# Four graph layers over a dense adjacency: int32 narrowed to bytes by GpSimd's converting transfers

## Chip, cores, metric

One core of a Trainium2 chip runs the whole program. The metric is device time in microseconds, median of the runs of a kernel. One further execution was profiled; every row quoted below is from it.

## What is computed

The input is x (8 graphs, 2048 nodes, 128 features, float32) and adj (8, 2048, 2048, int32, entries 0 or 1, each 1 with probability 0.0039). Four layers follow, each as x = x + layer(relu(layernorm(x)), adj):

```python
# layer 0: attention with 8 heads of 32, then one head of 128
e   = leaky_relu(f1[..., :, None] + f2[..., None, :], 0.2)
att = softmax(where(adj > 0, e, -9e15)); hp = elu(att @ h)      # twice, plus the input
# layer 1: maximum over a node's neighbours (itself left out)
cand = where(adj_without_diagonal > 0, h[:, None, :, :], -1e30)
out  = relu(norm(h @ W_self + cand.max(axis=2) @ W_neigh))
# layer 2: attention with 4 heads of 32
# layer 3: mean over the nodes that point here
pooled = (adj.T @ h) / counts;  out = leaky_relu(h @ B + pooled @ W, 0.1)
```

So all four layers of a graph need its adjacency: as a byte mask (layers 0, 2, 3) and as lists of each node's neighbours (layer 1).

## The kernel before

**Tiles.** A graph's adjacency is 16 tiles of 128 rows by 2048 columns, 1 MB a tile as int32. In SBUF it is held as bytes twice: `A` (rows) and `AT` (transposed), 16 tiles each.

**The load of a graph** (`load`, L382 to L390 on SyncE; `cast`, L760 to L772 on ScalarE; `transposed` on TensorE; `take` on VectorE). SyncE moves an int32 tile into one of two halves of the buffer `Rb` (L390), after a wait until ScalarE has done with that half. ScalarE reads it twice: L769 writes a bf16 copy and sums the row (the degree), L771 writes the byte copy with the value 56 into `A`. TensorE transposes the bf16 copy in 16 pieces (L1486), VectorE writes it to `AT` (L1148). `Rb` is also where the attention heads' rows lie, so SyncE begins a load only when the heads of layer 2 have ended. The loads of graphs 0 and 1 stand alone; those of graphs 2 to 7 are interleaved, one pair of tiles at a time, with the last layer of the graph two before.

**The software pipeline** (`pipeline`, L290). For each step b: `beside(b+1, b)` is the single wide head of layer 0 of graph b+1 with layer 1 of graph b woven in; `middle(b)` is layer 2 of graph b; `last_layer(b, b+2)` is layer 3 of graph b with the load of graph b+2; `heads_of(b+2)` is the eight heads of layer 0 of graph b+2. At the end come `beside(None, 7)`, `middle(7)` and `last_layer(7)`.

**The lists.** While the heads run, VectorE finds each node's neighbours eight at a time (`list_tile`, reading `A`), and SyncE or ScalarE stores the found numbers to DRAM (`lists`).

**The gather** (`gather`, L602 to L613, GpSimd). For each graph and each of its 16 tiles GpSimd fetches index lists (L543), fetches 128 rows per index with indirect transfers (L551, eight to a round, from `table` in DRAM, which holds layer 1's input), and takes maxima (L534 to L537); L595 writes the tile's result to `Agg`. GpSimd begins the gather of graph b when `table` has been written (semaphore `tab_in`, at the end of `beside(b, ...)`) and adds 1 to `maxima` at its end (L613). TensorE waits for `maxima` in `sage_arrived` (L1364), which in `sums` (L1379) comes after the second of the 16 tiles of `beside(b+1, b)`. One gather therefore runs beside all of `middle(b-1)`, `last_layer(b-1, b+1)`, `heads_of(b+1)` and the start of `beside(b+1, b)`.

All instructions of an engine run in the order written. GpSimd's queue of transfers is made by its software; SyncE's and ScalarE's are made by hardware. All three are moved by the same 16 DMA engines.

Of the kernel before, what the change touches and what calls it, by code (L numbers as in the profile page):

```python
# [31 lines left out]
ACT = mybir.ActivationFunctionType  # L32
# [3 lines left out]
U8, I8, U32, I32 = mybir.dt.uint8, mybir.dt.int8, mybir.dt.uint32, mybir.dt.int32  # L36

P = 128
# [5 lines left out]
ONE8 = 56  # L44
# [18 lines left out]
def build(nc, x, adj, W1, a1, W2, a2, Wself, bself, Wneigh, bneigh, gamma, beta, WC, aC, W3, B3, out):  # L63
    B, N, F = x.shape
    T = N // P
# [18 lines left out]
    with ExitStack() as ctx:  # L84
        def sb(name, shape, dt=F32):
            return ctx.enter_context(nc.sbuf_tensor(name, shape, dt))

        def sem(name):
            return ctx.enter_context(nc.semaphore(name))


        A = sb("A", [P, T, N], U8)
# [14 lines left out]
        Rb = sb("Rb", [P, 2, N])  # L107
# [20 lines left out]
        deg = sb("deg", [P, T])  # L128
# [23 lines left out]
        found_idx = sb("found_idx", [P, KEYS], U32)  # L152


        stage_i32 = Rb[:, :, :].bitcast(I32)
        f1row, f2row = Pbuf[0:8, 0, :], Pbuf[0:8, 1, :]
        xc = xcbuf[:, :].rearrange("p (t c) -> p t c", t=T)
        Dg = xcbuf[:, T * F:T * F + T * F // 2].bitcast(BF16).rearrange("p (t c) -> p t c", t=T)
        stage_bf = Pbuf[:, 0, :].bitcast(BF16).rearrange("p (u n) -> p u n", u=2)
# [25 lines left out]
        x1 = nc.dram_tensor("x1", [B, P, T * F], F32, kind="Internal").ap()  # L185
        h1 = nc.dram_tensor("h1", [B, P, T * F], F32, kind="Internal").ap()
        bytes_A = nc.dram_tensor("bytes_A", [B * T, P, N], U8, kind="Internal").ap()
        bytes_AT = nc.dram_tensor("bytes_AT", [B * T, P, N], U8, kind="Internal").ap()
        lists = nc.dram_tensor("lists", [ROUNDS + 2, P, KEYS], U32, kind="Internal").ap()
        h0 = nc.dram_tensor("h0", [P, T * F], F32, kind="Internal").ap()  # L190
# [17 lines left out]
        AT_in = sem("AT_in")  # L208
        adj_in = [sem("adj_in0"), sem("adj_in1")]
        cast_done = sem("cast_done")  # L210
        bf_done = sem("bf_done")
        at_ps = sem("at_ps")
        at_done = sem("at_done")
# [27 lines left out]
        keyed = sem("keyed")  # L241
# [9 lines left out]
        M = {m: {k: sem(f"{m}_{k}") for k in ("T", "hT", "W", "ev", "y")} for m in ("sage", "pool")}  # L251
# [15 lines left out]
        def plain(eng):  # L267

            eng.wait_ge(ready, 1)

        def settle(eng):

            eng.sem_inc(settled, 1)
# [43 lines left out]
        def _(sp):  # L317
# [22 lines left out]
            def tile_of(buffer, t):  # L340
                return buffer[:, bass.ds(t, 1), :].rearrange("p o c -> p (o c)")
# [39 lines left out]
            def load(b, alone):  # L381
                with sp.Fori(0, T // 2) as tt:  # L382
                    for u in range(2):
                        rows = x[bass.ds(b, 1), bass.ds(tt * (2 * P) + u * P, P), :].rearrange("o p f -> (o p) f")
                        sp.dma_start(tile_of(X, tt * 2 + u), rows).then_inc(x_in, 16)

                        plain(sp)
                        sp.wait_ge(cast_done, b * T + tt * 2 + (u + 1))
                        src = adj[bass.ds(b, 1), bass.ds(tt * (2 * P) + u * P, P), :].rearrange("o p n -> (o p) n")
                        sp.dma_start(stage_i32[:, u, :], src).then_inc(adj_in[u], 16)  # L390

            def heads_of(b, alone):

# [94 lines left out]
            def last_layer(b, following, alone):  # L488
                if following is not None:

                    plain(sp)
                    sp.wait_ge(S[LC]["pe"], b * (LC.H * T) + LC.H * T + free_P[LC])
                    settle(sp)
                    load(following, False)
                plain(sp)
                sp.wait_ge(x_done, b + 1)
                sp.dma_start(out[bass.ds(b, 1)].rearrange("o (t p) f -> p (o t) f", p=P), X2[:, :, :]).then_inc(out_done, 16)

            sp.sem_inc(out_done, 16)
            pipeline(sp, load, heads_of, beside, middle, last_layer)  # L500
            sp.wait_ge(out_done, B * 16 + 16)


        @block.gpsimd
        def _(pool):
# [33 lines left out]
            def fetch(r, slot):  # L539

                plain(pool)
                pool.wait_ge(list_in, r * 16 + 32)
                pool.dma_start(idx[:, slot, :], lists[bass.ds(r, 1)].rearrange("o p k -> (o p) k")).then_inc(idx_in[slot], 16)  # L543
# [11 lines left out]
            def number(b, t):  # L555
                return pool.value_load(cum[0:1, bass.ds(b * (T + 1) + t, 1)], min_val=0, max_val=ROUNDS)

            def tile(b, t, last):
                lo, hi = number(b, t), number(b, t + 1)

                fetch(lo if last else lo + 1, 1)
                rows_of(b * T + t + 1, 0, best)
                if last:

                    plain(pool)
                    pool.wait_ge(idx_in[1], lo * 16 + 16)
                pool.sem_inc(merged, MERGE)  # L570
                with pool.Fori(lo + 1, hi) as r:
                    if last:
                        fetch(r, 1)
                    rows_of(r + 1 if last else r, 1, G)
                    v = Chain(pool, merged, r * MERGE, MERGE)
                    for half in range(2):

                        plain(pool)
                        for k in range(half * KEYS // 2, (half + 1) * KEYS // 2):
                            pool.wait_ge(got[k], r * 16 + 16)  # L580
                        if half == 1 and not last:

                            fetch(r + 1, 1)
                        part = slice(half * KEYS // 2, (half + 1) * KEYS // 2)
                        greater(v, best[:, part, :], G[:, part, :])
                    v.end()
                    settle(pool)
                if not last:

                    fetch(hi, 0)  # L590
                v = Chain(pool, tree, (b * T + t) * TREE, TREE)
                for width in (4, 2, 1):
                    greater(v, best[:, 0:width, :], best[:, width:2 * width, :])
                settle(pool)
                v(pool.tensor_copy(Agg[:, bass.ds(t, 1), :].rearrange("p o f -> p (o f)"), best[:, 0, :]))  # L595
                v.end()
                if not last:

                    plain(pool)
                    pool.wait_ge(idx_in[1], hi * 16)  # L600
                settle(pool)

            def gather(b):

                plain(pool)

                pool.wait_ge(tab_in, b * 16 + 16)
                settle(pool)
                fetch(number(b, 0), 0)
                with pool.Fori(0, T - 1) as t:  # L610
                    tile(b, t, False)
                tile(b, T - 1, True)
                pool.sem_inc(maxima, 1)  # L613

            gather(0)
            if B > 1:
                with pool.Fori(0, B - 1) as b:

                    plain(pool)
                    pool.wait_ge(M["sage"]["T"], b * T + T)  # L620
                    gather(b + 1)


        @block.scalar
        def _(act):
# [135 lines left out]
            def cast(b, tt):  # L761

                for u in range(2):
                    n = b * T + tt * 2 + u
                    plain(act)
                    act.wait_ge(adj_in[u], (b * (T // 2) + tt + 1) * 16)

                    act.wait_ge(at_ps, n + 1)
                    act.activation(stage_bf[:, u, :], stage_i32[:, u, :],  # L769
                                   ACT.Copy, accum_out=deg[:, bass.ds(tt * 2 + u, 1)]).then_inc(bf_done, 1)  # L770
                    act.activation(A[:, bass.ds(tt * 2 + u, 1), :], stage_i32[:, u, :].rearrange("p (o n) -> p o n", o=1),  # L771
                                   ACT.Copy, scale=float(ONE8)).then_inc(cast_done, 1)  # L772

            def load(b, alone):
                with act.Fori(0, T // 2) as tt:
                    cast(b, tt)
# [775 lines left out]
```

## Time and profile before

| | before |
|---|---|
| median of 3 runs | 9315.55 us (9288.4 to 9319.17) |
| profiled execution, its own time | 9293.71 us |
| its span | 9292.0 us |
| mean granted clock of TensorE | 0.800 |
| TensorE busy | 5501.9 us (59%) |
| VectorE busy | 5998.1 us (65%) |
| ScalarE busy | 4627.4 us (50%) |
| GpSimd busy | 5119.1 us (55%) |
| bytes moved by DMA | 629.10 MB, mean 68 GB/s |

Busy time is the sum of an engine's instructions without its waits. No engine is busy over two thirds of the span, so the waits tell what bounds a stage: for each, the profile infers which instruction of another engine released it. The chain that ended last is followed back from the last instruction through these releases.

### The profile page before, as it was taken

The page shows a single profiled execution, that of the slowest core. Times are in us where ns is not written, and L with a number is a line of the kernel's source. Part 1 is how long each engine was busy: PE and PEld are TensorE (multiplying, and loading weights), DVE is VectorE, ACT ScalarE, POOL GpSimd, SP SyncE. Part 2 cuts the span into 40 slices and gives each one's busy share as a digit, 9 for nine tenths or more (in the row PEclk, how much of TensorE's full clock was granted, in tenths as well). Part 3 has the DMA queues.
Part 4 walks back from the last instruction along what each step waited for, and adds up shares of the span by engine and source line. Part 5 has one row for each costly group of instructions (what it writes and reads, how often), then busy time and mean ns, then how long its engine had stood idle before and what let it go on. Part 6 is the DMA issues. An engine that isn't in the chain of part 4 may idle for free.

```text
span 9292.0 us, 189286 instructions
## 1 busy us (share of the span) xinstructions
PE 5501.9 (59%) x62584; PEld 4902.1 (53%) x62584; DVE 5998.1 (65%) x7394; ACT 4627.4 (50%) x4624; POOL 5119.1 (55%) x5234
## 2 busy tenths in 40 slices
PE   3764670365776668564875668565775667562037
PEld 2663670363765547463864557454764557461026
DVE  4874871385876778685866778586866778581024
ACT  5643650165744557264845566355735566260034
POOL 0003777376753777376754676176764677277720
PEclk9886885687887889787987889787887888786568
DMA  2114332134332433235322533134323533222210
GB/s 97 38 38 109 68 71 24 31 69 124 61 65 58 105 79 61 50 64 134 65 59 66 120 65 75 51 63 107 66 60 67 119 64 77 56 52 55 27 22 28
DMA packets 305343, 629.10 MB, mean 68 GB/s; under 512 B 113273, under 2 KB 163962, under 8 KB 268666
## 3 DMA queue, kind: packets, MB, share of 16 engines
q0 software_dynamic: 91936, 161.87, 16.6%
q1 hardware_dynamic: 210514, 456.38, 13.9%
q8 instruction: 584, 9.57, 0.4%
q14 instruction: 149, 1.22, 0.0%
q10 hardware_dynamic: 2160, 0.06, 0.0%
HBM read 506.89 MB, written 111.15 MB: 67 GB/s over the span
## 4 chain that ended last, share of the span: by engine, by line
DVE 29%; PE 23%; issue 13%; ACT 7%; POOL 3%; DVEq 3%; DMA 2%; ACTq 2%; POOLq 0%; SPq 0%
PE ps L1419 7%; DVE keys L1095 4%; PE ps L1421 3%; PE ps L1444 3%; DVE key L1085 3%; PE ps L1333 3%; ACT Pbuf L700 2%; PE ps L1392 2%; PE ps L1330 2%; DVE key L1071 2%; ACT Hn L700 2%; DVE Hn L955 2%; DVE Zs L975 1%; DVE Zs L976 1%; DVE AT L1148 1%
## 5 line engine op out<-in xcount | busy, mean ns | idle before, releaser
L1421 PE MATMUL ps<-Hn,AT 128*128 128x99 bf16 x12288 | 1773.1, 216 | 0.0
L551 POOL DMA_INDIRECT G<-table,idx x1416 | 1493.0, 1054 | 504.4 <-issue 444.9
L1421 PE MATMUL ps<-X,AT 128*128 128x99 bf16 x12288 | 1738.0, 215 | 15.3 <-issue 15.3
L543 POOL DMA_DIRECT2D idx<-lists x433 | 259.3, 599 | 2644.6 <-issue 2164.8
L700 ACT ACTIVATE Hn<-Rb,q 128x2048 int8<-128x2048 f32 x768 | 1485.0, 1988 | 98.0 <-PE ps L1421 94.1
L700 ACT ACTIVATE Pbuf<-Rb,q 128x2048 int8<-128x2048 f32 x768 | 1487.2, 1987 | 12.7 <-PE ps L1421 10.3
L551 POOL DMA_INDIRECT best<-table,idx x1024 | 1109.0, 1083 | 319.5 <-issue 309.4
L1419 PE MATMUL ps<-X,Hn 128*128 128x198 bf16 x6144 | 938.2, 269 | 553.4 <-DVE Hn L955 318.1
L1421 PEld LDWEIGHTS ps<-Hn,AT 128*128 128x128 fp8e4 x12288 | 1256.3, 102 | 0.0
L1421 PEld LDWEIGHTS ps<-X,AT 128*128 128x128 fp8e4 x12288 | 1244.8, 101 | 16.5 <-issue 16.5
L1419 PE MATMUL ps<-Hn 128*128 128x198 bf16 x6144 | 960.3, 272 | 428.7 <-DVE Zs L975 243.1
L1419 PEld LDWEIGHTS ps<-X,Hn 128*128 128x128 fp8e4 x6144 | 652.4, 106 | 583.8 <-issue 567.0
L1419 PEld LDWEIGHTS ps<-Hn 128*128 128x128 fp8e4 x6144 | 660.5, 108 | 468.0 <-issue 448.2
L1419 PE MATMUL ps<-Hn,Pbuf 128*128 128x198 bf16 x6144 | 831.6, 252 | 66.0 <-DVE Pbuf L955 65.8
L1419 PE MATMUL ps<-X,Pbuf 128*128 128x198 bf16 x6144 | 820.0, 250 | 25.0 <-DVE Pbuf L955 25.0
L955 DVE SCALAR_TENSOR_TENSOR Hn<-Hn,AT 128x512 int32<-128x512 int32 x768 | 628.6, 847 | 216.5 <-ACT Hn L700 148.8
L955 DVE SCALAR_TENSOR_TENSOR Pbuf<-Pbuf,AT 128x512 int32<-128x512 int32 x768 | 633.6, 853 | 159.5 <-ACT Pbuf L700 126.9
L1095 DVE MAX8 keys<-key 128x8 f32<-128x2056 f16 x305 | 701.3, 2299 | 33.8 <-DVE key L1085 8.9
L1419 PEld LDWEIGHTS ps<-Hn,Pbuf 128*128 128x128 fp8e4 x6144 | 606.2, 99 | 79.3 <-issue 77.0
L729 ACT ACTIVATE hT<-ps 128x512 f32<-128x512 f32 x64 | 38.2, 597 | 1180.0 <-PE ps L1350 1180.0
L1419 PEld LDWEIGHTS ps<-X,Pbuf 128*128 128x128 fp8e4 x6144 | 601.9, 98 | 30.4 <-issue 29.8
L882 DVE COPY WHbuf<-ps 128x128 f32 (+1 forms) x384 | 129.1, 336 | 738.8 <-PE ps L1333 738.8
(190 smaller groups left out, 11639.4 us busy)
## 6 DMA issues: line engine op xcount, KB each, us to landing
Rb<-in_adj SPq DMA_DIRECT2D x128, 1024.0 KB
Rb<-rrows SPq DMA_DIRECT2D x104, 1024.0 KB, 6.5
bytes_A<-A SPq DMA_DIRECT2D x128, 256.0 KB
bytes_AT<-AT SPq DMA_DIRECT2D x128, 256.0 KB
AT<-bytes_AT SPq DMA_DIRECT2D x128, 256.0 KB
AT<-bytes_A SPq DMA_DIRECT2D x128, 256.0 KB, 3.6
G<-table,idx POOLq DMA_INDIRECT x1416
h<-Hn SPq DMA_DIRECT2D x16, 1024.0 KB, 4.2
```

The lines of the kernel that those rows point to most:

```text
L543: pool.dma_start(idx[:, slot, :], lists[bass.ds(r, 1)].rearrange("o p k -> (o p) k")).then_inc(idx_in[slot], 16)
L551: pool.indirect_dma_start(out=dst[:, k, :], out_offset=None, in_=table, in_offset=bass.IndirectOffsetOnAxis(ap=idx[:, slot, k:k + 1], axis ...
L700: act.activation(marks[(u * T + jb) % RING].bitcast(I8), Rb[:, u, :], ACT.Sign, bias=q[:, jb, hs], scale=-1.0).then_inc(s["sg"], 1)
L955: dve.scalar_tensor_tensor(marks[k % RING], marks[k % RING], NO_SIGN, A32, ALU.bitwise_and, ALU.bitwise_and).then_inc(s["p"], 1)
L1071: v(dve.scalar_tensor_tensor(key[:, 0:N], A[:, bass.ds(t, 1), :].rearrange("p o n -> p (o n)"), 0.0, iota[:, :], ALU.is_gt, ALU.mult))
L1085: dve.match_replace(key[:, :], keys8[:, :], key[:, :], 0.0).then_inc(removed, 1)
L1095: dve.max(keys8[:, :], key[:, :]).then_inc(found, 1)
L1330: pe.matmul(ps[:, 2 + u, 0:W], hT[:, u, k, :], w["cat"][:, k, :], start=k == 0, stop=k == L.KB - 1)
L1333: ins = pe.matmul(ps[0:L.H, 4 + u, e * P:(e + 1) * P], wf[:, k, :], hT[:, u, k, :], start=k == 0, stop=k == L.KB - 1)
L1419: pe.matmul(both[:, :, 0:G], greater[:, at], v.rearrange("p (g x) -> p g x", g=2), start=first, stop=False, skip_group_check=True)
L1421: ins = pe.matmul(both[:, 0, 0:G], A8[:, jb, at], v[:, 0:G], start=False, stop=jb == T - 1, skip_group_check=True)
L1444: ins = pe.matmul(ps[:, 4 + u, 0:3 * F + 1], A8[:, k, (tt * 2 + u) * P:(tt * 2 + u + 1) * P], PS3[:, k, 0:3 * F + 1], start=k == 0, stop=k ...
```

## The change

A second DRAM tensor `adj8` holds the adjacency as bytes. GpSimd issues, tile by tile, a transfer from `adj` (int32) to `adj8` (uint8) in DRAM (`narrow`), with at most two in flight, one for each of the semaphores `narrowed0` and `narrowed1`. Those of graphs 0 and 1 (32 tiles) are issued at the program's start, after GpSimd's constants. Those of graph b+2 (16 tiles) are issued in `gather(b)` for b = 0 to 5, after `tab_in` has been waited for and ahead of the first fetch. SyncE's load moves 256 KB a tile from `adj8` straight into `A`; it waits for `narrowed` and for its own transfer of the pair before, and no longer for ScalarE. The first seven pairs wait until the lists of the graph before but the last tile's are found (`keyed`), the last pair until all are. ScalarE's two passes read the byte tile in `A` in place of `Rb`; the second writes it in place. Nothing of the arithmetic of the layers changes.

```diff
+        adj8 = nc.dram_tensor("adj8", [B * T, P, N], U8, kind="Internal").ap()
...
+        narrowed = [sem("narrowed0"), sem("narrowed1")]
...
+                def pair(tt):
+                    for u in range(2):
                         plain(sp)
-                        sp.wait_ge(cast_done, b * T + tt * 2 + (u + 1))
-                        src = adj[bass.ds(b, 1), bass.ds(tt * (2 * P) + u * P, P), :].rearrange("o p n -> (o p) n")
-                        sp.dma_start(stage_i32[:, u, :], src).then_inc(adj_in[u], 16)
+                        sp.wait_ge(narrowed[u], b * (T // 2 * 16) + tt * 16 + 16)
+                        settle(sp)
+                        if not (alone and isinstance(tt, int) and tt == 0):
+                            plain(sp)
+                            sp.wait_ge(adj_in[u], b * (T // 2 * 16) + tt * 16)
+                            settle(sp)
+                        sp.dma_start(tile_of(A, tt * 2 + u), of(adj8, b * T + (tt * 2 + u))).then_inc(adj_in[u], 16)
+
+                if not alone:
+                    plain(sp)
+                    sp.wait_ge(keyed, b * (3 * T) - 3)
+                    settle(sp)
+                pair(0)
+                with sp.Fori(1, T // 2 - 1) as tt:
+                    pair(tt)
...
+                pair(T // 2 - 1)
...
+            def narrow(b, t, u):
+                rows = adj[bass.ds(b, 1), bass.ds(t * P, P), :].rearrange("o p n -> (o p) n")
+                pool.dma_start(adj8[bass.ds(b * T + t, 1)].rearrange("o p n -> (o p) n"), rows).then_inc(narrowed[u], 16)
+
+            def gather(b, ahead):
                 plain(pool)
                 pool.wait_ge(tab_in, b * 16 + 16)
                 settle(pool)
+                if ahead:
+                    with pool.Fori(0, T // 2) as tt:
+                        for u in range(2):
+                            plain(pool)
+                            pool.wait_ge(narrowed[u], (b + 2) * (T // 2 * 16) + tt * 16)
+                            settle(pool)
+                            narrow(b + 2, tt * 2 + u, u)
                 fetch(number(b, 0), 0)
...
+            for b in range(min(B, 2)):
+                for t in range(T):
+                    if b * T + t >= 2:
+                        pool.wait_ge(narrowed[t % 2], (b * T + t) // 2 * 16)
+                    narrow(b, t, t % 2)
...
-                    act.activation(stage_bf[:, u, :], stage_i32[:, u, :],
-                                   ACT.Copy, accum_out=deg[:, bass.ds(tt * 2 + u, 1)]).then_inc(bf_done, 1)
-                    act.activation(A[:, bass.ds(tt * 2 + u, 1), :], stage_i32[:, u, :].rearrange("p (o n) -> p o n", o=1),
-                                   ACT.Copy, scale=float(ONE8)).then_inc(cast_done, 1)
+                    tile = A[:, bass.ds(tt * 2 + u, 1), :].rearrange("p o n -> p (o n)")
+                    act.activation(stage_bf[:, u, :], tile, ACT.Copy, accum_out=deg[:, bass.ds(tt * 2 + u, 1)]).then_inc(bf_done, 1)
+                    act.activation(tile, tile, ACT.Copy, scale=float(ONE8)).then_inc(cast_done, 1)
```

What the program of GpSimd holds between `tab_in` and the first fetch of graph 0's gather (ISA rows carry the waits), before:

```order
L556 TENSOR_LOAD cum [waits ready,tab_in]
L556 ISA x2
L542 ISA [waits ready]
L543 ISA [waits list_in]
L543 DMA idx<-lists 128x8
```

and with the change (L636 is the loop over pairs, L627 the transfer to `adj8`):

```order
L636 UNCONDITIONAL_BRANCH [waits ready,tab_in]
L639 ISA [waits ready]
L627 ISA [waits narrowed0]
L627 REGISTER_ALU
L627 DMA adj<-in_adj 16x16384
L627 ISA [waits ready,narrowed1]
L627 REGISTER_ALU
L627 DMA adj<-in_adj 16x16384
L636 REGISTER_ALU
L636 COMPARE_AND_BRANCH
L577 TENSOR_LOAD cum
L577 ISA x2
```

Two waiting transfers of 16 pieces of 16384 numbers each, eight times over, now stand between `tab_in` and the fetch.

On SyncE, one tile of a load before (`X` is the features, `Rb` the staging buffer):

```order
L385 DMA X<-in_x 128x128
L388 REGISTER_ALU [waits ready]
L390 ISA [waits cast_done]
L390 DMA Rb<-in_adj 128x2048
L385 ISA
L385 DMA X<-in_x 128x128
```

and with the change, the first pair and the loop over the others:

```order
L397 DMA A<-adj 128x2048 [waits ready,narrowed0]
L397 DMA A<-adj 128x2048 [waits ready,narrowed1]
L405 UNCONDITIONAL_BRANCH
L391 ISA [waits ready]
L397 ISA [waits narrowed0,ready,adj_in0]
L397 DMA A<-adj 128x2048
L397 ISA [waits ready,narrowed1,adj_in1]
L397 DMA A<-adj 128x2048
```

The wait for `cast_done` is gone; the loads wait for the narrowing and for the load of the pair before.

## Rows read from the trace of the kernel before

**Rows 1.** The page: the chain that ended last, shares of the span by engine.

```profile
DVE 29%; PE 23%; issue 13%; ACT 7%; POOL 3%; DVEq 3%; DMA 2%; ACTq 2%; POOLq 0%; SPq 0%
```

**Rows 2.** Waits of TensorE: engine, line, releaser, then us in total, times, longest us.

```profile
PE ps L1349 <- POOLq L613: 796.0, 4, 461.9
```

**Rows 3.** Timeline of TensorE: start, us, operation, and in brackets the idle time before it.

```profile
1727.44 0.47 PE L1349 MATMUL ps<-ident,Hn 128*128 128x128 f32 x1 [320.63 <-POOLq L613]
...
2772.72 0.27 PE L1349 MATMUL ps<-ident,Hn 128*128 128x128 f32 x1
...
3825.91 0.47 PE L1349 MATMUL ps<-ident,Hn 128*128 128x128 f32 x1 [7.60 <-POOLq L613]
...
4834.88 0.27 PE L1349 MATMUL ps<-ident,Hn 128*128 128x128 f32 x1
...
5854.98 0.27 PE L1349 MATMUL ps<-ident,Hn 128*128 128x128 f32 x1
...
6929.09 0.47 PE L1349 MATMUL ps<-ident,Hn 128*128 128x128 f32 x1 [5.92 <-POOLq L613]
...
7960.72 0.27 PE L1349 MATMUL ps<-ident,Hn 128*128 128x128 f32 x1
```

**Rows 4.** Timeline of GpSimd: the first fetch of each graph's gather, same columns.

```profile
793.66 0.77 POOL L543 DMA_DIRECT2D idx<-lists  x1 [785.96 <-issue]
...
1853.37 0.60 POOL L543 DMA_DIRECT2D idx<-lists  x1 [126.52 <-issue]
...
2900.86 0.60 POOL L543 DMA_DIRECT2D idx<-lists  x1 [154.12 <-issue]
...
3951.36 0.62 POOL L543 DMA_DIRECT2D idx<-lists  x1 [126.02 <-issue]
...
4963.38 0.60 POOL L543 DMA_DIRECT2D idx<-lists  x1 [147.10 <-issue]
...
5990.80 0.60 POOL L543 DMA_DIRECT2D idx<-lists  x1 [211.14 <-issue]
...
7058.27 0.60 POOL L543 DMA_DIRECT2D idx<-lists  x1 [129.75 <-issue]
...
8094.22 0.60 POOL L543 DMA_DIRECT2D idx<-lists  x1 [139.51 <-issue]
```

**Rows 5.** Waits of GpSimd, columns as in Rows 2.

```profile
POOL idx L543 <- issue: 2164.8, 140, 786.0
...
POOL idx L543 <- DMA lists<-found_idx: 39.7, 24, 3.9
```

**Rows 6.** The page: DMA queues, their packets, MB, share of 16 engines' time.

```profile
q0 software_dynamic: 91936, 161.87, 16.6%
q1 hardware_dynamic: 210514, 456.38, 13.9%
```

**Rows 7.** By stretch: length, busy us (instructions) of PE, PEld, DVE, ACT, POOL; clock, DMA share, GB/s.

```profile
26.00:106.00 80.00, 26.42 (x225) 22.75 (x226) 34.86 (x28) 64.87 (x53) 0.00 (x0) 1.00 0.65 223
1853.00:1880.00 27.00, 12.67 (x72) 7.43 (x72) 14.28 (x29) 10.24 (x34) 19.14 (x20) 0.81 0.67 194
```

**Rows 8.** DMA issues by line: KB each, median us from issue to landing.

```profile
AT<-bytes_A SPq DMA_DIRECT2D x128, 256.0 KB, 3.6
...
idx<-lists POOLq DMA_DIRECT2D x433, 4.0 KB, 1.9
```

**Rows 9.** Timeline of ScalarE: the first and the last casts of graph 0's load.

```profile
30.64 1.28 ACT L769 ACT_TABLE_LOAD   x1 [30.50 <-DMA Rb<-in_adj]
...
102.56 1.28 ACT L769 ACT_TABLE_LOAD   x1 [1.70 <-DMA Rb<-in_adj]
...
109.45 1.89 ACT L771 ACTIVATE A<-Rb 128x2048 int32 x1
```

**Rows 10.** Timeline of GpSimd: the last of its constants.

```profile
7.50 0.20 POOL L530 CAST selfidx<-tmpi 128x16 f32<-128x16 int32 x1
```

**Rows 11.** The gather's line L551: duration in ns, least/median/most.

```profile
L551 POOL DMA_INDIRECT G<-table,idx x1416: 940/944/4882, 810.0 to 8893.5; - x177
```

More of the change, by code:

```diff
@@ L152, in build @@
         found_idx = sb("found_idx", [P, KEYS], U32)
-        stage_i32 = Rb[:, :, :].bitcast(I32)
         f1row, f2row = Pbuf[0:8, 0, :], Pbuf[0:8, 1, :]
@@ L385, in load @@
                         sp.dma_start(tile_of(X, tt * 2 + u), rows).then_inc(x_in, 16)
+                def pair(tt):
+                    for u in range(2):
                         plain(sp)
-                        sp.wait_ge(cast_done, b * T + tt * 2 + (u + 1))
-                        src = adj[bass.ds(b, 1), bass.ds(tt * (2 * P) + u * P, P), :].rearrange("o p n -> (o p) n")
-                        sp.dma_start(stage_i32[:, u, :], src).then_inc(adj_in[u], 16)
+                        sp.wait_ge(narrowed[u], b * (T // 2 * 16) + tt * 16 + 16)
[12 more added lines that the diff above has]
+                    pair(tt)
+                if not alone:
+                    plain(sp)
+                    sp.wait_ge(keyed, b * (3 * T))
+                    settle(sp)
+                pair(T // 2 - 1)
             def heads_of(b, alone):
@@ L601, in tile @@
                 settle(pool)
-            def gather(b):
+            def narrow(b, t, u):
+                rows = adj[bass.ds(b, 1), bass.ds(t * P, P), :].rearrange("o p n -> (o p) n")
+                pool.dma_start(adj8[bass.ds(b * T + t, 1)].rearrange("o p n -> (o p) n"), rows).then_inc(narrowed[u], 16)
+            def gather(b, ahead):
                 plain(pool)
@@ L613, in gather @@
                 pool.sem_inc(maxima, 1)
-            gather(0)
-            if B > 1:
-                with pool.Fori(0, B - 1) as b:
+            for b in range(min(B, 2)):
[3 more added lines that the diff above has]
+                    narrow(b, t, t % 2)
+            gather(0, B > 2)
+            if B > 3:
+                with pool.Fori(0, B - 3) as b:
                     plain(pool)
                     pool.wait_ge(M["sage"]["T"], b * T + T)
-                    gather(b + 1)
+                    gather(b + 1, True)
+            for b in range(max(B - 3, 0), B - 1):
+                plain(pool)
+                pool.wait_ge(M["sage"]["T"], b * T + T)
+                gather(b + 1, False)
         @block.scalar
```

## Prediction

> **What bounds the kernel now.** I read the chain of waits first. GpSimd has only 3% of it, which looks harmless [rows 1]. The waits of TensorE, sorted by total, say otherwise: its largest item by far is line 1349, the first transposition of layer 1, released by GpSimd's last instruction of a gather: 796.0 us in four waits [rows 2]. The chain gives this time to others, because it is followed through what GpSimd waited for in turn. So I looked at all eight meeting points of gather and main pipeline. The timeline of TensorE has the moment at which it passes each [rows 3], the timeline of GpSimd when each gather begins and how long GpSimd had idled before, so also when the gather before had ended [rows 4]: graph 1's ended at 2900.86 - 154.12 = 2746.74.
>
> - Graph 0: TensorE idles 320.63 us for the gather, from 1406.8 to 1727.4.
> - Graphs 2 and 5: it idles 7.60 and 5.92 us [rows 3].
> - Graph 7: the rest of the 796.0, 461.9 us [rows 2].
> - Graph 1: ended at 2746.7, needed at 2772.7. With 0.6 us to hand over (graph 0: ended at 1853.37 - 126.52 = 1726.85, used at 1727.44) 25 us are spare.
> - Graph 3: ended at 4816.3, needed at 4834.9, 18 us spare. Graph 4: 5779.7 against 5855.0, 75 us spare. Graph 6: 7954.7 against 7960.7, 5 us spare.
>
> The reader is to see that between two meeting points two strands of nearly equal length run side by side, the main pipeline and the gather, and that the gather is the longer or within 75 us of it each time. The gather itself lasts 816 to 938 us (4963.4 to 5779.7, and 5990.8 to 6928.5) [rows 4], and little in it can give: it waited for lists only 39.7 us in the whole run, 3.9 at most [rows 5]. The next gather cannot begin before the meeting, since the table is written in the same `beside`. Whatever is put in front of a gather adds to its strand in full.
>
> **The change, part by part.**
>
> *Narrowing ahead of six gathers (graphs 0 to 5).* GpSimd may not fetch before it has issued 16 transfers, each after the second last has landed. So it is held for about the transfers' own time, N. This is priced from rows of other transfers, as none here converts. One tile reads 1.049 MB. In the load of graph 0 the engines moved 223 GB/s at a share of 0.65, that is 343 GB/s when busy [rows 7]: 3.06 us a tile. The latency does not bind: issue 0.60 [rows 4], 1.9 us to landing for a small transfer on this queue [rows 8] and 3.06 of data make 5.6 us for each of two slots, 2.8 a tile. Sixteen tiles are 49 us. In the same stretch SyncE restores `AT` and spreads the heads' rows: 27 us with 194 GB/s at a share of 0.67 are 18 us of full engines [rows 7], served in turn with the narrowing. With 1 us for the last issue **N = 68 us**.
>
> The lower bound is the hardware queue's mean: 456.38 MB in 13.9% of 16 engines' time, 353 GB/s, 2.97 us a tile, with the other traffic fitting into gaps: N = 47.5. The upper bound is the mean of GpSimd's own queue: 161.87 MB in 16.6%, 105 GB/s [rows 6], 9.98 us a tile, with 18 us beside it: N = 178. That queue's rate comes from rows of 512 bytes; the narrowing moves 64 KB a piece, as SyncE's large loads do or more, so I take the price near the low end.
>
> The Trainium skill, page "DMA: Bandwidth & Descriptors", section on the anatomy of a DMA on the gpsimd path, fits 2.0 us plus bytes/436e3 us for one transfer. By that, as an estimate, a tile's data are 2.4 us, N is 39 us without other traffic, and the sum below would be 140 us, still slower; the stretch read here shows 343 GB/s, not 436, and neither shows a conversion.
>
> *What N costs.* A period is the longer of the two strands: each pays N less its spare time. Graph 0: 68, graph 2: 68, graph 5: 68, graph 1: 68 - 25 = 43, graph 3: 68 - 18 = 50, graph 4: 68 - 75, nothing. Sum 297 us. Gathers 6 and 7 narrow nothing. (In short: 5N - 43 up to N = 75, 6N - 118 above.)
>
> *The start.* GpSimd's constants end at 7.7 us [rows 10], so narrowing leads. Graph 0's casts ran from 30.64 to 111.3; every pair but the first waited some 1.5 us for its 1 MB transfer (1.70 in the last) [rows 9], seven times, 10.5 us. A 256 KB transfer lands 3.6 us after issue [rows 8] and SyncE is now several tiles ahead; the first tile comes about 1.5 us earlier (25.5 + 3.6 against 30.6). **Minus 12 us.** The last tile is narrowed at about 8 + 16 x 3.1 = 58 us, well before its cast; only above about 5.5 us a tile would the start be paced by narrowing.
>
> *ScalarE's passes.* Both read bytes where they read int32, with as many instructions and elements. No row has a byte source of this size. I take the same 1.9 us [rows 9]. If they took half, some 61 us would be saved in each load; but in five of six narrowing periods the gather is then the longer strand and the saving buys nothing. At the start ScalarE's 61 us could shrink until VectorE's and TensorE's share binds: up to 30 us more.
>
> *The loads of graphs 1 to 7.* Their waits for int32 tiles vanish, and the spare bytes too (16 MB become 4 MB in SBUF traffic). All of this lies on the main strand, which is the shorter one with the change, but for graph 4 (7 us apart, either way) and graph 6 (5 us spare, so the main strand counts; only a few us of waits). Zero, with the longer gather as cover; without that cover it would be worth a few us a load.
>
> *The middle's beginning.* `AT` and the heads' rows now share the engines with the narrowing, up to 18 us later on the main strand. The same cover hides it, save in graph 4: 0 to 10 us. Taken as zero.
>
> *`keyed`.* SyncE waits for lists that were stored in the heads before, and for the last list ahead of the last pair. Behind it in SyncE's queue stands only the store of the output, needed much later. Zero.
>
> Sum: 297 - 12 = 285 us over the profiled execution's own 9293.71: 9578.7. The median of the runs lies 21.8 us above that execution, so **9600 us**.
>
> **Rivals.**
>
> *The conversion is slow (5 to 10 us a tile).* For it: nothing in the trace converts, and GpSimd's queue shows 105 GB/s [rows 6]. Against it: that is small rows. At 9.98 us, N = 178, 6 x 178 - 118 = 950; the start is paced by narrowing, last tile at 8 + 160, landed and cast by about 176 instead of 111, plus 65: 9315.6 + 1015 = 10,331. At 7.8 us (N = 143) it is 740 + 30 above, 10,086.
>
> *The gather absorbs it (not slower).* If GpSimd's gather were paced by the lists, a later start would cost nothing, and the total would be 12 us lower at the start and a few in each load: about 9290. For it: GpSimd idles 2164.8 us with no releaser named [rows 5]. Against it: 786 + 126.5 + 154.1 + 126.0 + 147.1 + 211.1 + 129.8 + 139.5 = 1820 of these lie ahead of the gathers [rows 4], the rest is 2.6 us at each of the other 132 fetches, and the named waits for lists are 39.7 us. It decides only if slack in a gather exceeds N.
>
> *GpSimd's issuing is held up.* Gather transfers take 944 ns at the median but up to 4882 [rows 11]. If each of the 16 issues took 4.9 us in GpSimd, N would be 16 x 4.9 = 78 us or a little more: 6 x 78 - 118 - 12 = 338, 9654. The Trainium skill, page "SBUF — State Buffer", box on the "DVE blocks DMA" trap, says that GpSimd cannot write descriptors while VectorE holds the shared port; the longest gathers agree with that, but the median shows it to be rare.
>
> *Element by element.* If the conversion broke the pieces into single numbers, a tile would cost 16384 pieces an engine. GpSimd's queue took 24,680 engine-us for 312,320 gathered rows, 0.08 us each: 1.3 ms a tile, 0.1 s in all. The order shows whole runs of 16384, so this is unlikely.
>
> **How the numbers follow.** Likeliest, N of 47 to about 95 us: 0.68, of which 0.05 is held-up issuing. Slow conversion 0.20, of which 0.12 below 7.8 us. Absorbed 0.04. Element by element or worse than 10 us 0.08. The likeliest case's own range is 9480 to 9750. N = 47.5 gives 194.5 - 12 = 182.5, 9476 in the profiled execution's terms; the low end is 9470. Upwards the range goes to 10,090 (7.8 us a tile), which leaves out the rest of the slow case (0.08), the extreme (0.08) and the absorbed case (0.04). A measurement of this kernel can tell about 0.3%, 28 us. Faster needs the absorbed case with a ScalarE gain: 0.02. Same: 0.02. Slower: 0.96.
>
> **What would show it.** TensorE's wait at the meeting should appear for six graphs with about 390, 43, 75, 50, 0 to 5 and 74 us for graphs 0 to 5, and again some 460 for graph 7. On GpSimd a gap of N between a narrowing's first transfer and the gather's first fetch; gather lengths from there unchanged. ScalarE's casts at 1.9 us, with no wait for int32 tiles; the first load over some 12 us earlier. Wrong would be: a wait for `maxima` that does not grow, narrowing transfers over 5 us apart, or a gather that becomes shorter by what stands before it.

## The result, and the profile after

| | before | with the change |
|---|---|---|
| median | 9308.38 us (4 runs) | 9527.3 us (4 runs, 9512.64 to 9550.3) |
| ratio | | 1.0238 (95% interval 1.0223 to 1.0253) |
| profiled execution, own time | 9293.71 us | 9512.64 us |
| span | 9292.0 us | 9511.1 us |
| bytes moved | 629.10 MB | 562.20 MB |
| GpSimd busy | 5119.1 us | 5172.4 us |

The change makes the kernel 2.4% slower, 219 us in the profiled execution, though the page counts 67 MB less and the compute engines do nearly the same work (GpSimd 53 us more). The waits of TensorE show where the time is; this is the row that answers to [rows 2]:

```profile
PE ps L1392 <- POOLq L646: 993.0, 6, 451.0
```

The wait for the gather has grown from 796.0 us in four places to 993.0 in six. (The page's chain breaks off after 3% of the span in this trace and is not read.) The timeline of TensorE at the eight meeting points, in the order of [rows 3]:

```profile
1778.47 0.47 PE L1392 MATMUL ps<-ident,Hn 128*128 128x128 f32 x1 [337.20 <-POOLq L646]
...
2850.40 0.47 PE L1392 MATMUL ps<-ident,Hn 128*128 128x128 f32 x1 [32.33 <-POOLq L646]
...
3944.54 0.47 PE L1392 MATMUL ps<-ident,Hn 128*128 128x128 f32 x1 [71.46 <-POOLq L646]
...
4997.75 0.47 PE L1392 MATMUL ps<-ident,Hn 128*128 128x128 f32 x1 [31.92 <-POOLq L646]
...
6026.36 0.27 PE L1392 MATMUL ps<-ident,Hn 128*128 128x128 f32 x1
...
7144.75 0.47 PE L1392 MATMUL ps<-ident,Hn 128*128 128x128 f32 x1 [69.11 <-POOLq L646]
...
8173.05 0.27 PE L1392 MATMUL ps<-ident,Hn 128*128 128x128 f32 x1
...
9121.83 0.45 PE L1392 MATMUL ps<-ident,Hn 128*128 128x128 f32 x1 [450.99 <-POOLq L646]
```

Graphs 0, 1, 2, 3 and 5 now wait for their gather. Where 25 and 18 us were spare for graphs 1 and 3, 32.3 and 31.9 us of waiting stand; graphs 2 and 5 went from 7.6 and 5.9 us to 71.5 and 69.1. Graph 4 is still met by the main pipeline last.

On GpSimd, the head of the gathers of graphs 1 and 2 (compare [rows 4]):

```profile
1902.92 0.58 POOL L627 DMA_DIRECT2D adj<-in_adj  x1 [125.01 <-issue]
1903.80 0.53 POOL L627 DMA_DIRECT2D adj<-in_adj  x1 [0.30 <-issue]
1910.05 0.49 POOL L627 DMA_DIRECT2D adj<-in_adj  x1 [5.71 <-DMA adj<-in_adj]
1912.76 0.49 POOL L627 DMA_DIRECT2D adj<-in_adj  x1 [2.22 <-issue]
...
1962.86 0.49 POOL L627 DMA_DIRECT2D adj<-in_adj  x1 [3.63 <-issue]
1964.41 0.57 POOL L564 DMA_DIRECT2D idx<-lists  x1 [1.07 <-issue]
...
2976.36 0.58 POOL L627 DMA_DIRECT2D adj<-in_adj  x1 [126.53 <-issue]
...
3036.74 0.56 POOL L564 DMA_DIRECT2D idx<-lists  x1 [1.06 <-issue]
```

Each pair of transfers waits for the pair before; the first fetch comes 1964.41 - 1902.92 = 61.5 us after the first narrowing. For the six gathers this delay N is 55.2, 61.5, 60.4, 60.0, 59.0 and 60.3 us. A transfer lands 7.0 us after its issue (median; the 256 KB are its written bytes):

```profile
adj<-in_adj POOLq DMA_DIRECT2D x128, 256.0 KB, 7.0
```

The queues, against [rows 6]:

```profile
q0 software_dynamic: 96032, 195.43, 19.7%
q1 hardware_dynamic: 210514, 355.72, 10.7%
```

GpSimd's queue has 33.6 MB more (the written bytes of 128 tiles) and 4096 packets more, 32 a tile or two for each engine. Its time went from 16.6% of 9292 us to 19.7% of 9511 us: 16 engines times 331 us, over 128 tiles 2.6 us a tile. The same difference gives 2.6 to 3.0 us in the kernels of experiments 1, 2, 3 and 5, so I read it as an estimate with that spread. The conversion is thus done at no less than the pace of the int32 loads (3.06 us in the prediction), and in long pieces.

The 67 MB are a matter of what is counted. This is the HBM line of the page, the one of before first:

```profile
HBM read 506.89 MB, written 111.15 MB: 67 GB/s over the span
```

```profile
HBM read 540.45 MB, written 144.71 MB: 72 GB/s over the span
```

The loads read 100.7 MB less than before and the narrowing reads 134.2 MB: together the 33.6 MB that the first number grew by. The queue's row counts only the narrowing's 33.6 MB of written bytes. So with the change more bytes are read from and written to DRAM than before, not fewer.

And the start, which was to be 12 us shorter. SyncE and ScalarE at the first load (compare [rows 9]):

```profile
26.07 25.08 SPq L386 DMA_DIRECT2D X<-in_x  x16
51.45 56.21 SPq L397 DMA_DIRECT2D A<-adj  x16
```

```profile
56.88 1.28 ACT L814 ACT_TABLE_LOAD   x1 [56.75 <-DMA A<-adj]
...
58.18 1.91 ACT L814 ACTIVATE Pbuf<-A 128x2048 bf16 x1
...
65.69 1.28 ACT L814 ACT_TABLE_LOAD   x1
```

SyncE takes 25.08 us to issue the 16 feature tiles and only then issues the first load of `A`; ScalarE's first cast is at 56.88 in place of 30.64. From there the pairs follow each other every 8.8 us without a wait, in place of 10.1 us before, and a byte source takes ScalarE the same 1.91 us as an int32 one. So of the 26.2 us that the first cast is late, the eight pairs give back 10, and the last cast ends 16.0 us later than before (127.3 against 111.3). GpSimd's queue of work for gather 0 begins at 808.22, 14.6 us after 793.66.

**Where the 219 us come from.** G is a gather from its first fetch to its last instruction, N the delay before it.

| graph | N | G before | G after | meeting before | meeting after | added in this period | forecast |
|---|---|---|---|---|---|---|---|
| 0 | 55.2 | 933.2 | 914.5 | 1727.4 | 1778.5 | 51.0, of it start 14.6 | 68 - 12 |
| 1 | 61.5 | 893.4 | 885.4 | 2772.7 | 2850.4 | 26.6 | 43 |
| 2 | 60.4 | 924.5 | 907.2 | 3825.9 | 3944.5 | 41.0 | 68 |
| 3 | 60.0 | 864.9 | 867.3 | 4834.9 | 4997.8 | 44.2 | 50 |
| 4 | 59.0 | 816.3 | 821.8 | 5855.0 | 6026.4 | 8.5 | 0 |
| 5 | 60.3 | 937.7 | 921.8 | 6929.1 | 7144.8 | 44.3 | 68 |
| 6 | | 896.4 | 891.0 | 7960.7 | 8173.1 | -3.3 | 0 |
| 7 | | 815.3 | 812.7 | 8909.8 | 9121.8 | -0.3 | 0 |
| end | | | | 9292.0 | 9511.1 | 7.0 | 0 |

The 7 us at the end are not the change's. The last stage of both, the one of before first (columns as in [rows 7]), and then of the kernel before in its second profile (experiment 4):

```profile
8909.00:9292.00 383.00, 238.86 (x2612) 202.67 (x2612) 161.94 (x307) 194.35 (x225) 0.37 (x2) 0.82 0.08 26
```

```profile
9121.00:9511.10 390.10, 245.56 (x2612) 205.33 (x2612) 161.94 (x307) 194.41 (x225) 0.45 (x2) 0.80 0.08 25
```

```profile
8946.30:9336.10 389.80, 245.25 (x2612) 207.83 (x2612) 162.14 (x307) 194.59 (x225) 0.00 (x0) 0.80 0.08 25
```

The same 2612 multiplications took 238.86 us at a mean granted clock of 0.82 and 245.56 at 0.80, and the kernel before has both: 382.2 us from its last meeting to the end in one execution, 389.8 in the other.

### The profile page after: what moved, and what is told of

Its sections match the earlier page's. It is cut to its first block and busy times, and to the rows that moved or that the text cites. A ratio compares the mean times of both kernels' runs of the same rounds, so it can differ in the third digit from the quotient of the medians.

```text
span 9511.1 us, 190248 instructions
## 1 busy us (share of the span) xinstructions
PE 5493.1 (58%) x62584; PEld 4892.2 (51%) x62584; DVE 5992.3 (63%) x7394; ACT 4626.1 (49%) x4624; POOL 5172.4 (54%) x5362
## 2 busy tenths in 40 slices
DMA packets 309466, 562.20 MB, mean 59 GB/s; under 512 B 115321, under 2 KB 166010, under 8 KB 287098
## 3 DMA queue, kind: packets, MB, share of 16 engines
q0 software_dynamic: 96032, 195.43, 19.7%
## 5 line engine op out<-in xcount | busy, mean ns | idle before, releaser
L1464 PE MATMUL ps<-Hn,AT 128*128 128x99 bf16 x12288 | 1778.5, 216 | 0.0
L627 POOL DMA_DIRECT2D adj<-in_adj x128 | 64.2, 501 | 1747.8 <-issue 1457.9
L969 DVE SCALAR_TENSOR_TENSOR Pbuf<-Rb,q,AT 128x2048 f32<-128x2048 f32 x128 | 305.1, 2386 | 660.8 <-PE ps L1435 639.4
```

Of the source, the lines that this page charges most:

```text
L627: pool.dma_start(adj8[bass.ds(b * T + t, 1)].rearrange("o p n -> (o p) n"), rows).then_inc(narrowed[u], 16)
L969: dve.scalar_tensor_tensor(tiles_P[jb % 2], Rb[:, slot, :], q[:, jb, h], AT[:, jb, :], ALU.max, ALU.mult).then_inc(s["p"], 1)
L1464: ins = pe.matmul(both[:, 0, 0:G], A8[:, jb, at], v[:, 0:G], start=False, stop=jb == T - 1, skip_group_check=True)
```

## The experiments

All but the fourth and the fifth start from the changed kernel; the seventh joins two edits. Times are medians with the ratio to the kernel before on the same chip.

**1. The narrowing in the gap.** The six narrowings move from the head of a gather to its end, behind `maxima`.

```diff
-                if ahead:
-                    with pool.Fori(0, T // 2) as tt:
...
                 fetch(number(b, 0), 0)
...
                 pool.sem_inc(maxima, 1)
+                if ahead:
+                    with pool.Fori(0, T // 2) as tt:
...
```

> The narrowing of graph b+2 moves from the head of gather(b) to its end, into the gap of 125 us and more in which GpSimd waits for the next table. Theory (each period is the longer of two strands, and GpSimd holds the gather back by N = 60 us): TensorE's waits for the gather fall back to some 320, 0, 0 to 8 and so on; six gaps between a gather's first fetch and its table vanish; time 9290 to 9325, within 0.3% of before, since the start stays 15 us later than before and the gathers keep their shortening of up to 19 us. Rival (the narrowing's traffic itself slows the kernel, wherever GpSimd issues it): at least 9480.

Measured: 9319.87 us, ratio 1.0005 (0.9989 to 1.002). The whole loss is gone, although the first gather still begins 17.6 us later than before (811.26 against 793.66); the six gathers are 38 us shorter together. Two stretches of GpSimd's timeline, then TensorE's wait:

```profile
1733.14 0.29 POOL L616 COPY Agg<-best 128x128 f32<-128x128 f32 x1 [0.16 <-issue]
1734.79 0.58 POOL L627 DMA_DIRECT2D adj<-in_adj  x1 [1.35 <-issue]
...
1793.23 0.49 POOL L627 DMA_DIRECT2D adj<-in_adj  x1 [3.00 <-issue]
1859.86 0.56 POOL L564 DMA_DIRECT2D idx<-lists  x1 [66.13 <-issue]
```

```profile
PE ps L1392 <- POOLq L639: 789.7, 3, 461.8
```

The transfers start 1.4 us after the gather's last instruction and are all issued by 1793.7, 66 us before the next table is ready. The same bytes are converted, by the same engine, in the same number of transfers; only the place differs. The rival, that the traffic itself is the price wherever it runs, is out.

**2. One in flight.** In the gather each transfer waits for the one just before it.

```diff
-                            pool.wait_ge(narrowed[u], (b + 2) * (T // 2 * 16) + tt * 16)
+                            pool.wait_ge(narrowed[1 - u], (b + 2) * (T // 2 * 16) + tt * 16 + u * 16)
```

> In the gather each narrowing transfer waits for the one just before, so one is in flight in place of two. A transfer landed 7.0 us after its issue with two in flight, 5.3 at least. Theory: N grows from 60 to about 16 x 6.2 = 100 us, five periods pay 40 us more and that of graph 4 pays what exceeds its 21 us of spare time, 19: 9527 + 219 = 9746. Rival (N is nothing but bytes on busy engines, 16 x 2.6 us and 18 us of other traffic): N and the time stay, 9527.

Measured: 9752.78 us, ratio 1.0477 (1.0455 to 1.0498), 7 us from the forecast. N is 98.5 to 106.8 us. The head of graph 1's gather:

```profile
1952.41 0.58 POOL L627 DMA_DIRECT2D adj<-in_adj  x1 [127.41 <-issue]
1959.52 0.54 POOL L627 DMA_DIRECT2D adj<-in_adj  x1 [6.53 <-DMA adj<-in_adj]
```

A gather's delay passes into the total one for one, less the spare time. N is also not merely bytes: with the same bytes it is 45 us longer on average.

**3. All at once.** GpSimd issues the 16 transfers without a wait between them, after one wait for all earlier ones; SyncE's loads of graphs 2 to 7 wait until all 16 tiles have landed.

```diff
                 if ahead:
+                    for u in range(2):
+                        plain(pool)
+                        pool.wait_ge(narrowed[u], (b + 2) * (T // 2 * 16))
+                    settle(pool)
                     with pool.Fori(0, T // 2) as tt:
                         for u in range(2):
-                            plain(pool)
-                            pool.wait_ge(narrowed[u], (b + 2) * (T // 2 * 16) + tt * 16)
-                            settle(pool)
```

> In the gather all 16 narrowing transfers are issued at once; SyncE waits for all of a graph's before its load. Theory (the gather is held back by bytes: 16 x 2.6 us on the engines and 18 us of other traffic): the issuing takes 10 us, but the first index lists land behind the queue, so the meetings stay where they were, 9500 to 9530. Rival (GpSimd's waits between the transfers are the price): five periods give back 45 us each, 9300.

Measured: 9498.24 us, ratio 1.0202 (1.0174 to 1.0231), 2 us below the window I gave and far from the rival's 9300. The head of graph 0's gather in this run, then in the changed kernel:

```profile
813.47 0.49 POOL L630 DMA_DIRECT2D adj<-in_adj  x1 [691.75 <-issue]
814.25 0.49 POOL L630 DMA_DIRECT2D adj<-in_adj  x1 [0.30 <-issue]
...
827.36 0.49 POOL L630 DMA_DIRECT2D adj<-in_adj  x1 [0.24 <-issue]
829.05 0.57 POOL L567 DMA_DIRECT2D idx<-lists  x1 [1.20 <-issue]
...
857.63 1.04 POOL L575 DMA_INDIRECT best<-table,idx  x1 [25.92 <-DMA idx<-lists]
```

```profile
808.22 0.49 POOL L627 DMA_DIRECT2D adj<-in_adj  x1 [689.77 <-issue]
...
865.53 0.54 POOL L564 DMA_DIRECT2D idx<-lists  x1 [1.53 <-issue]
869.42 1.04 POOL L572 DMA_INDIRECT best<-table,idx  x1 [3.35 <-DMA idx<-lists]
```

GpSimd has issued everything after 15 us, but then waits 25.92 us for the index list queued behind it. From the first narrowing to the first row of the gather: 857.63 - 813.47 = 44.2 us here, 869.42 - 808.22 = 61.2 in the changed kernel. Over the six gathers it is 44 to 47 us against 61 to 69. Before, the fetch of the lists alone took 6.2 us there (graph 0) or under 4. So some 38 to 43 us of the delay stay with everything in the queue, which is what 16 tiles of 2.6 us make, and 17 to 23 us come from having only two in flight.

The kernel gained little by it: 1.0202 against the changed kernel's 1.0238, with intervals that overlap. TensorE's waits for graphs 1 to 5 fell to 4, 27, 5, 0 and 31 us, but its own strand became 12 to 31 us longer in each of these periods. What lengthened it was not traced; SyncE's transfers stood beside the full queue too (the last section has their times). The rival had counted the gather's strand alone.

**4. The kernel before, profiled once more** (no edit), to learn how much a gather's length differs from execution to execution.

> The kernel before once more, for a second profile. The six gathers that follow a narrowing in the changed kernel lasted 5370 us together before and 5318 with the change. Theory (the shortening comes from the smaller loads): 5360 to 5380 again. Rival (it lies within what executions differ by): a sum 20 us or more away from 5370.

Measured: the six gathers lasted 935.7 + 893.9 + 925.8 + 859.3 + 814.6 + 941.0 = 5370.3 us. One by one they differ by up to 6 us from the first profile, in sum by 0.3. The changed kernel's 5318 thus lies well outside what two executions of one kernel differ by. (One run, 9337.73 us, not compared.)

**5. The old load beside the narrowing.** The kernel before, with `adj8`, the 32 narrowings at the start and the six at the gathers' heads as in the change; the loads stay int32 from `adj`, and nobody reads `adj8`.

```diff
+            def narrow(b, t, u):
...
-            def gather(b):
+            def gather(b, ahead):
...
+                if ahead:
+                    with pool.Fori(0, T // 2) as tt:
...
+                            narrow(b + 2, tt * 2 + u, u)
```

> The kernel before with the narrowing added as in the change and its result unused: loads of 1 MB of int32 a tile into the staging buffer, as before. Theory (the gathers became shorter because the loads became smaller): gathers as long as before, N of 60 us and 80 us for graph 0 (16 MB of int32 beside it), the start 20 us later: 9311 + 80 + 35 + 60 + 42 + 0 + 60 + 20 = 9608. Rival (they became shorter because they begin later, after the middle's transfers): 50 us less, 9555.

Measured: 9629.78 us, ratio 1.0352 (1.0321 to 1.0384), 22 us above the forecast and further from the rival's 9555. The gathers sum to 920.4 + 900.7 + 914.7 + 879.0 + 836.1 + 940.1 = 5391 us, 73 more than with byte loads. N of graph 0 is 60.0 us, not the 80 I had priced, and the start is 844.34 - 793.66 = 50.7 us later, not 20. ScalarE's first two pairs:

```profile
41.92 1.28 ACT L794 ACT_TABLE_LOAD   x1 [41.79 <-DMA Rb<-in_adj]
...
61.52 1.28 ACT L794 ACT_TABLE_LOAD   x1 [7.63 <-DMA Rb<-in_adj]
```

A pair takes 19.6 us instead of 10, as the load's transfers share the engines with the narrowing. A late begin does not shorten the gathers: here they are 21 us longer than before. That the smaller loads do it is what remains of the two explanations, with the limits named below.

**6. The feature tiles interleaved.** In SyncE's load the transfer of each feature tile goes back beside that of its adjacency tile.

```diff
-                with sp.Fori(0, T // 2) as tt:
-                    for u in range(2):
-                        rows = x[...]
-                        sp.dma_start(tile_of(X, tt * 2 + u), rows).then_inc(x_in, 16)
                 def pair(tt):
                     for u in range(2):
+                        rows = x[...]
+                        sp.dma_start(tile_of(X, tt * 2 + u), rows).then_inc(x_in, 16)
```

> The change as it is, but the feature tiles are moved between the adjacency tiles again, as before the change, and not all 16 ahead of them. Theory (SyncE's 16 feature transfers, 25 us, hold up the first load of A in graph 0): ScalarE's first cast at about 31 us in place of 56.9, gather 0's narrowing begins 26 us earlier, time 9501. Rival (the narrowing of the first tiles holds up the start): first cast later than 45 us, time 9527.

Measured: 9531.12 us, ratio 1.0244 (1.0223 to 1.0264): no gain in the total. ScalarE's first cast, and SyncE's first four transfers of the load:

```profile
38.12 1.28 ACT L811 ACT_TABLE_LOAD   x1 [37.99 <-DMA A<-adj]
```

```profile
28.84 0.38 SPq L386 DMA_DIRECT2D X<-in_x  x1
29.34 1.60 SPq L394 DMA_DIRECT2D A<-adj  x1
31.00 0.43 SPq L386 DMA_DIRECT2D X<-in_x  x1
31.54 3.50 SPq L394 DMA_DIRECT2D A<-adj  x1
```

The first cast did move, from 56.9 to 38.1, but not to 31: a 256 KB load issued at 29.34 lands near 38, not after 3.6 us [rows 8], beside the narrowing. Gather 0's narrowing began at 794.17, 14 us earlier. But N of graph 0 was 3.5 us longer and its gather 11.6, so TensorE passed the first meeting at 1779.6 against 1778.5. The six gathers summed to 5343 us, 25 more than in the changed kernel. Why interleaved feature tiles should lengthen gathers was not tried.

**7. Gap and interleaving together.**

> Both: the narrowing in the gap and the feature tiles interleaved. Theory: the two gains add, 26 us below the kernel with the gap alone, 9265 to 9300, faster than before by up to 0.5%. If the shortening of the gathers came from their later begin and not from the smaller loads, 9295 to 9300. Rival (traffic): 9450 or more.

Measured: 9286.82 us (10 runs), ratio 0.9974 (0.9958 to 0.9989). TensorE's wait for the gather, beside [rows 2]:

```profile
PE ps L1389 <- POOLq L636: 806.2, 4, 456.9
```

This is the fastest kernel of the study, 33 us below experiment 1, where 26 were expected. Against the kernel before it is 0.26% faster: the interval leaves out 1, but the gain is far below 2%. Its first gather begins at 789.73, 21.5 us earlier than in experiment 1; the six gathers sum to 5346 us, 13 more. Where the rest of the 33 us comes from was not traced.

**8. Spread over the gather.** One narrowing at the head of each of the gather's 16 tiles. These and graph 1's count on a semaphore of their own, `ahead_done`, on which SyncE's loads of graphs 1 to 7 wait.

```diff
+                if ahead:
+                    plain(pool)
+                    pool.wait_ge(ahead_done, b * (T * 16) + (t * 16 + T * 16))
+                    settle(pool)
...
+                    pool.dma_start(adj8[bass.ds((b + 2) * T + t, 1)].rearrange("o p n -> (o p) n"), rows).then_inc(ahead_done, 16)
                 lo, hi = number(b, t), number(b, t + 1)
```

> One narrowing transfer at the head of each of the gather's 16 tiles (graphs 2 to 7; the wait there is for the one a tile before, long landed). Theory (only GpSimd's time counts): each costs some 0.8 us of issuing, so a gather becomes 13 us longer; 9320 of the kernel with the narrowing in the gap and three times 13 us: 9340 to 9370. Rival (a narrowing costs its 2.6 to 3.7 us of transfer wherever it stands beside a gather, since the gather's rows share the engines): 16 x 3.7 = 60 us a gather, 9500.

Measured: 9339.23 us, ratio 1.0029 (1.0013 to 1.0044), a hair below the 9340 to 9370 that the theory gave. The head of graph 1's gather:

```profile
1871.50 0.62 POOL L568 DMA_DIRECT2D idx<-lists  x1 [124.96 <-issue]
1872.81 0.56 POOL L589 DMA_DIRECT2D adj<-in_adj  x1 [0.69 <-issue]
1874.94 0.58 POOL L568 DMA_DIRECT2D idx<-lists  x1 [1.57 <-issue]
1875.82 1.02 POOL L576 DMA_INDIRECT best<-table,idx  x1 [0.31 <-issue]
```

The transfer stands between two fetches and the gather doesn't wait for it. The six gathers sum to 5421 us against 5332 in experiment 1: 15 us each, a quarter of the block at the head, and about the 13 us that 16 issues were expected to cost GpSimd. The sums of the other kernels with byte loads lie up to 38 us apart, 6 us a gather, so the 15 us are no sharper than that.

## Why the prediction was right, and where its sizes were off

The time was forecast at 9600 and measured at 9527.3, inside the range of the likeliest case (9480 to 9750). The mechanism was right; the size was not: 285 us were added up and 219 measured. N came out too long (43 us over the five periods that it was charged to), the gathers became shorter (58 us in these periods), and the start went the other way by 27 us, which by luck covers part of the first two. By its steps:

- **Two strands, and the gather holds.** Right, and shown from three sides: moved into the gap the loss is gone (experiment 1), with N raised to 104 us the total rises by what the spare times leave (9753 measured, 9746 expected), and the waits appear at the five meetings named. They were forecast at 390, 43, 75, 50 and 74 us and are 337, 32, 71, 32 and 69. Graph 0's is the furthest off, as TensorE itself arrived 34.5 us later than before (1441.3 against 1406.8): 14.6 of these are the start, the other 20 lie on its own strand beside the narrowing, like the "up to 18 us" of the middle's beginning, and the gather's wait covered them.
- **N = 68 us.** Measured 55 to 62. Two errors of opposite sign. A tile's data were priced at 3.06 us from int32 loads and 18 us of other traffic was added on top; the queue's share gives 2.6 us, and with all in flight 16 tiles and the traffic beside them took 44 us up to the first row. But "the latency does not bind" was wrong: it used the 1.9 us of a small transfer, while with one in flight the issues follow each other only every 6.5 to 7.0 us on average (experiment 2), and two in flight cost 17 to 23 us over everything at once. With two in flight a tile took 3.6 to 4.0 us, not 2.8.
- **"Gather lengths unchanged."** This is the largest miss: in the four periods 0, 1, 2 and 5 the gathers were 60 us shorter together. I had counted the smaller loads as worth something only on the main strand. A likely cause is that they also free the engines that the gather's rows use: within graph 2's gather, GpSimd's waits for rows ahead of an index fetch went from 45.0 us (15 times) to 23.5 (10 times). In graphs 0, 1 and 5 they fell by 9.7, 15.6 and 2.3 us. The sums of the six gathers support it: 5370, 5370 and 5391 us with int32 loads (before, experiments 4 and 5), 5308 to 5346 with byte loads (the changed kernel, experiments 1, 2, 6 and 7). It is not settled: the gather of graph 6 has a load of the new kind beside it and nothing ahead of it in each of these kernels, and it lasted 879 to 910 us against 896 and 898 before.
- **The start, minus 12.** Wrong in sign: plus 14.6. The 10.5 us of waits between pairs did vanish. The step that failed is "SyncE is now several tiles ahead", with the first tile 1.5 us earlier: the first cast came 26.2 us later. The diff puts all 16 feature tiles before the first `A` tile, and I did not price their issuing. It took 25.1 us while the narrowing filled the engines; see the last section.
- **ScalarE's passes at 1.9 us.** Right. The alternative beside it was added up wrongly: 61 us are all 32 passes of a load, and half of that is 30. It entered no sum.
- **Graph 4 and the later stages, zero.** 8.5 us in graph 4's period, which I had given 0 to 10; -3.6 in the periods of graphs 6 and 7, and 7.0 at the end, at a lower clock that the kernel before shows too.
- **Rivals.** The slow conversion is out (2.6 to 3.0 us of the engines a tile). GpSimd's issues were not held up: 486 ns at the median, 1151 at most. The trap of which the Trainium skill warns on the page "SBUF — State Buffer" (descriptors that GpSimd cannot write while VectorE holds the port) did not show in them.
- **The page's fit.** Of the fit in the Trainium skill's page "DMA: Bandwidth & Descriptors" (anatomy section), the 2.4 us of data for a tile is closer to the measured 2.6 than my 3.06, but its 4.4 us for a lone transfer of 1 MB is short of the 4.8 us of the quickest with one in flight, and of the 5.8 us at the median (experiment 2). The estimate of 140 us from it was further off the measured 219 than my 285.

## What to carry to other kernels

Before adding work to an engine with 3% of the chain, compare for each meeting of two strands when both sides arrive: a strand that is ready 18 us before it is needed is as good as critical for a 60 us block. Work that can be done at any time belongs in the engine's own gap (here 125 us between two gathers, with no loss left in the total) or, second best, one piece at a time between its steps (15 us), and not in a block ahead of them (60 us). A semaphore chain with two in flight is no proof of full overlap: here it cost 17 to 23 us a block. But filling the queue instead hardly paid, as the other strand slowed.

## What the runs showed of the hardware

**Issuing slows beside another queue's large transfers.** Sixteen transfers of 64 KB from SyncE took 25.08 us to issue at the start, with the narrowing beside them. The same 16 in the load of graph 1, in the changed kernel (two narrowing transfers in flight), in experiment 1 (none beside them) and in experiment 3 (all 16 in the queue at once):

```profile
806.98 17.89 SPq L386 DMA_DIRECT2D X<-in_x  x16
```

```profile
809.63 12.09 SPq L386 DMA_DIRECT2D X<-in_x  x16
```

```profile
812.29 41.93 SPq L386 DMA_DIRECT2D X<-in_x  x16
```

With one in flight it was 20.86 us (experiment 2). Where and how the narrowing is issued is what differs between these kernels, so it is the cause: these hardware transfers are issued at 0.3 to 0.7 of their pace beside it, and what stands behind them in SyncE's order pays. It is not the engines' busy share alone, which was 0.59 with one in flight and 0.90 with two. In experiment 6, where the feature tiles are issued one by one between other transfers, the first ones took 0.38 and 0.43 us.

**The conversion in DRAM costs no more than the int32 loads did.** From int32 to bytes, 1 MB read and 256 KB written, it took 2.6 to 3.0 us of the engines a tile, an estimate by difference from the queue's share; a plain copy of the same kind was not run. In the queue's row the profile counts its written bytes only, and in the HBM line its read bytes in full: experiment 5, which adds the 128 narrowings and leaves the loads alone, reads 641.11 MB against 506.89, 134.2 more.
